# Opening of a fast-weight layer in another order on four engines, with the router's choice woven into its first steps

## The reference, cut to what matters

```python
xn = _layernorm(x)
xq, xk, xv = xn @ wq, xn @ wk, xn @ wv            # 16 heads of 64, chunks of 64 tokens
# for each chunk, state W and bias bb carried along:
lr = sigmoid(xk_c @ theta + tb);  eta = token_eta * lr / HD
Z1 = xk_c @ W + bb;  x_hat = (Z1 - mu) / std
grad_output = g * x_hat + be - (xv_c - xk_c)
Wn, bn = W - dW, bb - db                          # from eta and the gradient through the norm
out = xq_c + g * norm(xq_c @ Wn + bn) + be
# experts: softmax over tokens, the 32 strongest tokens of each expert
logits = einsum('bsd,de->bse', xn, Wg) + bg;  vals, idx = top_k(softmax(logits, -2).T, 32)
```

## Time and profile before

| what | value |
|---|---|
| median of 3 runs | 970.23 us (970.03 to 971.91) |
| the profiled execution's own time | 971.49 us |
| its span, first to last instruction | 969.3 us |
| busy: PE, DVE, ACT, POOL | 894.1, 781.8, 555.2, 629.6 us |
| mean granted TensorE clock | 0.979 |

### The profile page before, as it was taken

One profiled execution on the slowest core, in us unless ns is written; L12 is line 12 of the kernel. 1 busy time (PEld: TensorE's weight loads), 2 busy tenths in 40 slices (PEclk: granted clock), 3 DMA queues, 4 the chain that ended last, 5 costly groups with the idle time before them and its releaser, 6 DMA issues.

```text
span 969.3 us, 19700 instructions
## 1 busy us (share of the span) xinstructions
PE 894.1 (92%) x7768; PEld 617.4 (64%) x7768; DVE 781.8 (81%) x1182; ACT 555.2 (57%) x828; POOL 629.6 (65%) x571
## 2 busy tenths in 40 slices
PE   1687999999998897799999999999999999999997
PEld 1555778777786677556556656656656656666664
DVE  7768988998897635787887897888798788888876
ACT  3453666666664361456657656666655765756663
POOL 3357887888885002777668669568767866955872
PEclk9998999999999899799999999999999999999999
DMA  8100000000000301211011102101211111220110
GB/s 224 29 2 1 2 2 3 2 3 2 3 3 1 88 2 62 58 44 64 21 45 64 65 19 69 64 4 61 66 31 55 64 36 32 74 75 20 45 50 23
DMA packets 24962, 38.25 MB, mean 39 GB/s; under 512 B 9316, under 2 KB 15480, under 8 KB 22824
## 3 DMA queue, kind: packets, MB, share of 16 engines
q1 hardware_dynamic: 23240, 34.74, 11.7%
q10 hardware_dynamic: 1632, 2.27, 0.8%
HBM read 28.29 MB, written 1.43 MB: 31 GB/s over the span
## 4 chain that ended last, share of the span: by engine, by line
PE 60%; DVE 18%; issue 11%; POOL 6%; ACT 3%; DMA 1%; SPq 0%; POOLq 0%; DVEq 0%
PE bank L1142 12%; PE bank L1144 10%; PE bank L1143 10%; DVE hdh L958 5%; PE bank L1406 3%; PE bank L1298 3%; PE quad L1437 3%; PE quad L1194 3%; DVE add L967 2%; DVE mx L951 2%; PE quad L1185 2%; POOL arena L1068 2%; PE quad L1342 2%; PE bank L1257 2%; POOL arena L1062 2%
## 5 line engine op out<-in xcount | busy, mean ns | idle before, releaser
L951 DVE TENSOR_REDUCE mx<-quad 128x4 f32<-128x2048 f32 x64 | 146.4, 2288 | 41.4 <-PE quad L1437 41.3
L1113 POOL CAST hdh<-xn 128x512 fp32r<-128x512 f32 x96 | 65.7, 685 | 138.3 <-ACT xn L620 138.3
L635 ACT ACTIVATE ex<-quad 128x2048 f32<-128x2048 f32 x64 | 120.6, 1885 | 58.7 <-PE quad L1447 58.7
L1115 POOL TENSOR_TENSOR hdl<-hd,hdh 128x512 fp32r<-128x512 f32 x96 | 129.9, 1353 | 7.7
L1115 POOL TENSOR_TENSOR hdl<-xn,hdh 128x512 fp32r<-128x512 f32 x96 | 128.6, 1339 | 7.7
L1142 PE MATMUL bank<-hdh,W2h 128*128 128x512 f32 x256 | 113.1, 442 | 6.3 <-DVE hdl L961 4.1
L620 ACT ACTIVATE xn<-bank,b1c 128x512 f32<-128x512 f32 x128 | 88.0, 687 | 35.2 <-POOL hdl L1115 18.7
L620 ACT ACTIVATE hd<-bank,b1c 128x512 f32<-128x512 f32 x112 | 77.0, 688 | 45.1 <-PE bank L1144 26.8
L1144 PE MATMUL bank<-hdl,W2h 128*128 128x512 f32 x256 | 100.7, 393 | 0.0
L1143 PE MATMUL bank<-hdh,W2l 128*128 128x512 f32 x256 | 100.5, 393 | 0.0
L1142 PE MATMUL bank<-cH,W1h 128*128 128x512 f32 x192 | 81.0, 422 | 0.7 <-DVE cL L978 0.7
(11 more groups left out here) (304 smaller groups left out, 2205.5 us busy)
## 6 DMA issues: line engine op xcount, KB each, us to landing
cwB<-gate_rows SPq DMA_DIRECT2D x16, 1024.0 KB, 4.7
kx<-kqh SPq DMA_DIRECT2D x32, 64.0 KB, 2.1
qx<-kqh SPq DMA_DIRECT2D x32, 64.0 KB, 2.1
ex<-in_L_ffn_W SPq DMA_DIRECT2D x1, 1024.0 KB, 5.7
kx<-kql SPq DMA_DIRECT2D x16, 64.0 KB, 2.1
qx<-kql SPq DMA_DIRECT2D x16, 64.0 KB, 2.1
rec<-rec_rows SPq DMA_DIRECT2D x32, 32.0 KB, 2.1
out<-fin SPq DMA_DIRECT2D x4, 256.0 KB, 2.3
```

The source lines that it names most:

```text
L635: act.activation(ex[:, t % 2, :, :], quad[:, :, :], ACT.Exp, scale=float(AD) ** -0.5).then_inc(ROUND["exps_ready"], 1)
L951: dve.tensor_reduce(mx[:, t, :, 0], quad[:, :, :], AX_X, ALU.max, negate=True).then_inc(ROUND["score_max"], 1)
L1113: pool.tensor_copy(hdh[:, m % RING, :], tile(n)).then_inc(ROUND["pool_split"], 1)
L1115: pool.tensor_tensor(hdl[:, m % RING, :], tile(n), hdh[:, m % RING, :], ALU.subtract).then_inc(ROUND["pool_split"], 1)
```

## The change

It touches nothing behind the fast-weight loop. In words:

- GpSimd: clears `wgP` at the start (VectorE did); multiplies `theta` first, as soon as theta and `wk` are loaded; subtracts `wkl` only once the layer norm is done; no longer writes half of `Wst`; multiplies `wu` by gamma only once VectorE has written all of `Wst`; copies the router's weights into `wgP` ahead of `wql`.
- VectorE: casts `pair` and `ones` ahead of the norm; theta's sum and the bias come before `Wst`, of which it writes all four batches; scaling of the rates (`rates_scaled`) moves behind xhat of step 0; the pieces of the choice move from the end of steps 0 to 3 to two places within steps 1 to 4, one behind `xhat` and one ahead of L795.
- ScalarE: two of the four key blocks move into steps 0 and 1; the square root's table is loaded right behind the sigmoid and right behind the exponential, each by a one-element activation; the exponential moves from step 1 to step 2.
- TensorE: the same two key blocks move into steps 0 and 1; the router's logits go to `bank[0]` and wait for `wgP` alone; the turning of `wq` moves from step 0 to step 1 and waits for `choice(0)`; the turning of the ranks moves from step 4 to step 5; the first state products wait for `Wst` by halves.

The core of the diff:

```diff
             act.wait_ge(gamma_loaded, 16)
             act.activation(gg[:, :], gamB[:, :], ACT.Square, scale=HD ** -0.5).then_inc(wu_high, 1)
-            act.wait_ge(wu_ready, 2)
-            act.activation(wuh[:, :], wu[:, :], ACT.Copy, scale=1.0 / HD).then_inc(wu_high, 1)
...
-            for m in range(4):
-                keys(m, m + 1, second_bank if m % 2 else first_bank)
+            keys(0, 1, first_bank)
             act.wait_ge(bias_placed, 1)
             act.activation(Bhl[:, :], db_[:, :], ACT.Copy).then_inc(bias_first_high, 1)
+            keys(1, 2, second_bank)
+            act.wait_ge(wu_ready, 2)
+            act.activation(wuh[:, :], wu[:, :], ACT.Copy, scale=1.0 / HD).then_inc(wu_high, 1)
...
             act.activation(eta[:, :, :, :], eta[:, :, :, :], ACT.Sigmoid).then_inc(rates_sigmoid, 1)
-            act.wait_ge(target_ready, 1)
+            act.activation(warm[:, :], C("ln_eps"), ACT.Sqrt)
...
+                if s == 2:
                     act.wait_ge(choice_step, 2)
                     act.activation(rkp[:, 1, :], lgt[:, :], ACT.Exp, bias=es[:, 0:1], accum_out=es[:, 1:2]).then_inc(choice_exp, 1)
-                if s == 2:
+                    act.activation(warm[:, :], C("ln_eps"), ACT.Sqrt)
...
             for s in range(4 * NC + 6):
-                centre(s - 1), sum_squares(s), sum_squares_q(s), rdev(s), xhat(s), rdev_q(s)
+                centre(s - 1), sum_squares(s), sum_squares_q(s), rdev(s), xhat(s)
+                if s == 0:
+                    rates_scaled()
+                elif s <= 4:
+                    choice(2 * s - 2)
+                rdev_q(s)
                 if s % 2:
                     bias_low((s - 3) // 2)
-                normed(s), rate_of(s - 1), gradient(s), update(s - 2), sum_gx(s), sum_gx_xhat(s)
-                if s == 0:
-                    choice(0), choice(1)
-                elif s == 1:
-                    choice(2), choice(3)
-                elif s == 2:
-                    choice(4), choice(5)
-                elif s == 3:
-                    choice(6)
+                normed(s), rate_of(s - 1), gradient(s), update(s - 2), sum_gx(s)
+                if 1 <= s <= 4:
+                    choice(2 * s - 1)
+                sum_gx_xhat(s)
...
                 if s == 0:
-                    pe.wait_ge(wg_ready, 1)
-                    pe.wait_ge(rates_biased, 1)
+                    pe.wait_ge(CHUNK["u_taken"], 1)
+                    features(first_bank, 2, 0, wkh, wkl).then_inc(CHUNK["keys_ready"], 1)
+                    pe.wait_ge(wg_ready, 2)
                     for b in range(B):
-                        last = pe.matmul(misc[0:BE, :], wgP[:, b, :], xnT[:, b * S:(b + 1) * S], start=(b == 0), stop=(b == B - 1))
+                        last = pe.matmul(bank[0][0:BE, :], wgP[:, b, :], xnT[:, b * S:(b + 1) * S], start=(b == 0), stop=(b == B - 1))
                     last.then_inc(choice_logits, 1)
+                if s == 1:
+                    pe.wait_ge(CHUNK["xk_taken"], 2)
+                    features(second_bank, 3, 0, wkh, wkl).then_inc(CHUNK["keys_ready"], 1)
+                    pe.wait_ge(choice_step, 1)
```

More of the change, by code:

```diff
@@ L537, in _ @@
                 if s == 0:
+                    keys(2, 3, first_bank)
+                if s == 1:
+                    keys(3, 4, second_bank)
                     act.wait_ge(wq_turned, 1)
@@ L655, in _ @@
             half_ = lambda t: t.unsqueeze(2).broadcast_to([P, 8, P])
+            dve.wait_ge(consts_loaded, 16)
+            dve.tensor_copy(pair[:, :], C("pair"))
+            dve.tensor_scalar(ones[:, :], ident, 0.0, 1.0, ALU.mult, ALU.add)
             for k in range(2):
@@ L677, in _ @@
                 dve.tensor_tensor(by_chunk(xtl, b), bank[b][:, :].rearrange("p (i c) -> p i c", c=K), by_chunk(xth, b), ALU.subtract).then_inc(CHUNK["tokens_low"], 1)
[L679 to L682, removed]
+            dve.wait_ge(theta_scaled, 1)
+            dve.tensor_reduce(Th[:, :], th[:, :].rearrange("p (h c) -> p h c", h=H), AX_X, ALU.add).then_inc(theta_ready, 1)
             dve.wait_ge(rows_loaded, 16 * 8)
@@ L687, in _ @@
             dve.tensor_tensor(b8, b8, mb[:, 1, :].unsqueeze(2).broadcast_to([P, 8, HD]), ALU.subtract).then_inc(bias_ready, 1)
-            dve.wait_ge(consts_loaded, 16)
-            dve.tensor_copy(pair[:, :], C("pair"))
-            dve.tensor_scalar(ones[:, :], ident, 0.0, 1.0, ALU.mult, ALU.add)
+            dve.wait_ge(w_mean_ready, 1)
+            for b in range(B):
+                dve.tensor_tensor(Wst[:, b, :, :], W1s[:, :, :], m0[:, 1, 0:NP].unsqueeze(2).broadcast_to([P, NP, HD]),
+                                  ALU.subtract).then_inc(weights_centred, 1)
+            dve.wait_ge(bias_first_high, 1)
+            dve.scalar_tensor_tensor(out=Bhl[:, :], in0=Bhl[:, :], scalar=C("low_minus"), in1=db_[:, :], op0=ALU.mult, op1=ALU.add).then_inc(bias_ready, 1)
             link(dve.scalar_tensor_tensor(out=gb2[:, 0, :], in0=gb2[:, 0, :], scalar=1.0 / HD, in1=gb2[:, 1, :], op0=ALU.mult, op1=ALU.mult))
@@ L693, in _ @@
             dve.tensor_tensor(gbr[32:33, :], gb2[32:33, 0, :], gbr[32:33, :], ALU.subtract).then_inc(target_ready, 1)
-            dve.wait_ge(bias_first_high, 1)
-            dve.scalar_tensor_tensor(out=Bhl[:, :], in0=Bhl[:, :], scalar=C("low_minus"), in1=db_[:, :], op0=ALU.mult, op1=ALU.add).then_inc(bias_ready, 1)
+            dve.wait_ge(small_loaded, 16 * 4)
+            link(dve.tensor_scalar(rate[:, :], alpha[:, :], C("token_rate"), 0.0, ALU.add, ALU.max))
+            dve.tensor_scalar(rate[:, :], rate[:, :], 1.0 / HD, None, ALU.mult)
             dve.wait_ge(wu_high, 2)
             dve.scalar_tensor_tensor(out=wul[:, :], in0=wu[:, :], scalar=1.0 / HD, in1=wuh[:, :], op0=ALU.mult, op1=ALU.subtract).then_inc(wu_low, 1)
[L698 to L703, removed]
-                last = dve.tensor_copy(wgP[:, b, b * E0:(b + 1) * E0], wg0[:, :])
-            last.then_inc(wg_ready, 1)
-            for j in range(4):
-                r = slice(32 * j, 32 * j + 32)
-                dve.tensor_copy(b3s[r, :], eb[r, 2, :].rearrange("p (g j) -> p j g", j=4)[:, j, :])
-            dve.wait_ge(small_loaded, 16 * 4)
-            link(dve.tensor_scalar(rate[:, :], alpha[:, :], C("token_rate"), 0.0, ALU.add, ALU.max))
-            link(dve.tensor_scalar(rate[:, :], rate[:, :], 1.0 / HD, None, ALU.mult))
             dve.wait_ge(rates_raw, 1)
@@ L1050, in _ @@
             pool.wait_ge(gamma_loaded, 16)
+            pool.wait_ge(weights_centred, B)
             pool.tensor_tensor(wu[:, :], wu[:, :], gamB[:, :], ALU.mult).then_inc(wu_ready, 1)
+            pool.wait_ge(moe_loaded, 16 * N_M)
+            pool.wait_ge(wg_ready, 1)
+            for b in range(B):
+                last = pool.tensor_copy(wgP[:, b, b * E0:(b + 1) * E0], wg0[:, :])
+            last.then_inc(wg_ready, 1)
             pool.wait_ge(wq_high, 1)
```

63 lines of the change are left out of this document (34 added, 29 removed).

## The result

The changed kernel takes 961.15 us (median of 4 runs, 955.78 to 961.82), the kernel before 970.61 in the same rounds; the ratio of the means is 0.9889 with a 95% interval of 0.9852 to 0.9926 (that of the medians is 0.990; the one run at 955.78 makes the difference). The profiled execution took 961.21 us, its span is 959.2 us. The prediction was 960.0, with 956.0 to 963.5 as its range.

A forecast was written before the change was run, and what follows sets the result against it. No engine was full; a chain of hand-overs bound it, with GpSimd products blocking VectorE. Norm -4.1, theta +2.1, rest of opening -7.2, then +1.7, -4.4 and +1.7 gave -10.2: 970.2 to 960.0 us, range 956.0 to 963.5.

The forecast's parts named there:

- Theta (+2.1): Opening: GpSimd's theta product starts first and blocks VectorE's second subtraction, a loss of 2.1 us.
- rival A: Opening: VectorE starts first at theta, so the 2.1 us loss is absent; 957.9 us (956 to 959), chance 0.30.
- The norm (-4.1): End of the layer norm: with `wkl` waiting, VectorE's last products take 1.29 instead of 5.43 us, a gain of 4.1.
- The rest of the opening (-7.2): Opening apart from theta and norm: a gain of 7.2 us, with xhat of step 0 at 41.5 instead of 50.7.
- the two further blocks foreseen: Opening: VectorE held by GpSimd's gamma product for 1.4 us, and `wul` by `wql` for 2.2 us.
- GpSimd's four copies: Opening: copies into `wgP` between 30.1 and 32.2 us, free up to 2.1 us; if longer, `wul` precedes `wql`.
- a free GpSimd product: Opening: a GpSimd product over 1024 columns by itself, taken as 2.2 us.
- The table load: Opening, ScalarE: 1.3 us without the page's drain; by the page xhat of step 0 would come 1.4 us later.
- Step 0 to 1 (+1.7): Keys and logits wait for ScalarE's target copy; 1.7 us lost, the gain falling from 9.2 to 7.5.
- Rival B: Steps 0 and 1: TensorE stays at 1.2 GHz, xhat of step 1 at 55.5 not 52.2; 963.3 us, chance 0.17.
- Steps 1 to 5 (-4.4, +1.7): From xhat of step 1: moving the choice gains 4.4 us; step 4 to 5, with scan and passes new, loses 1.7.

The follow-up runs named there:

- wkl_early: The changed kernel with GpSimd's `wkl` no longer waiting for the norm: 962.6 us, 0.9921 of the kernel before.
- wql_late: The changed kernel with GpSimd's `wql` waiting until VectorE's `wul` is made: 957.0 us, 0.9852 of the kernel before.
- wst_gpsimd: The changed kernel with half of `Wst` (last two batches) back on GpSimd, TensorE's first state products waiting for all of it: 959.8 us, 0.9896 of the kernel before.
- logits_twice: The changed kernel with the router's logits computed twice in a row: 962.0 us, 0.9917 of the kernel before.
- choice_old: The changed kernel with VectorE's pieces of the choice back at the end of steps 0 to 3: 961.4 us, 0.9918 of the kernel before.
- mean_first: The changed kernel with GpSimd's `wkl` waiting for L680 (the mean of W1) instead of the norm: 958.0 us, 0.9864 of the kernel before.
- before_wait: The kernel before with only GpSimd's `wkl` made to wait for the norm: 971.5 us, 1.0006 of the kernel before.
- theta_late: The changed kernel with GpSimd's theta product also waiting for VectorE's second subtraction: 959.2 us, 0.9883 of the kernel before.
- before_choice5: The kernel before with choice and exponential placed as in the change, TensorE's turning of the ranks and ScalarE's copy in step 5: 964.4 us, 0.994.
- all_three: The changed kernel with theta behind VectorE's second subtraction, `wkl` behind L680, `wql` behind `wul`: 953.5 us, 0.9831 of the kernel before.

## Why the prediction was right

**Theta (+2.1).** Right in place and size (3.28 less 1.22 is 2.1). That it fell as forecast was luck: with the same code up to this point, GpSimd was first in five profiles (changed, wkl_early, wql_late, wst_gpsimd, logits_twice) by 0.01 to 0.14 us, and VectorE in two (choice_old by 0.10 us; mean_first, where theta landed 1.2 us behind VectorE's start). So rival A's mechanism exists; whether the changed kernel's one run of 955.8 us is such a case, its time alone doesn't tell.

**The norm (-4.1).** Right to the tenth, and wkl_early undid it. But before_wait shows that it is worth nothing alone. That it pays here because the other products were moved and thinned out as well fits the rows of before_wait, but no run divides the two.

**The rest of the opening (-7.2).** It was -6.3: xhat of step 0 came at 42.4 and not 41.5. The mis-sized step is "`wkl` then runs to 21.6 beside VectorE's `xtl`, which reads PSUM": ahead of `xtl` stands L680 with an SBUF input, which waited 1.7 us, so `xtl` ended at 23.8 and not 22.5. mean_first shows it. The Trainium skill, "SBUF — State Buffer", section "Who interferes with whom", counts `tensor_scalar` and `cast` among the VectorE instructions that can, under conditions on their operands, take the ports shared with GpSimd, and this trace agrees (1.90 us for L680). I had asked only for two inputs in SBUF. Of the two further blocks foreseen, 1.4 and 2.2, the profile has 1.4 and 1.7 (2.57 and 2.93 us less a free 1.2). GpSimd's four copies took 2.07 us and `wql` still began ahead of `wul`, as assumed. The 2.2 us that I took for a free GpSimd product was a little short: it measured 2.34 to 2.37, and the earlier trace rows already had 2.35.

The table load again took 1.28 us and the next activation started 1.30 us after it (38.59, 39.89), so the figure of the trace held. The 2.66 us that the Trainium skill, "ScalarE: Activation LUTs", section "What ACT_TABLE_LOAD costs", gives for a load with its drain were not seen here either.

**Step 0 to 1 (+1.7).** It gave back 1.6: 10.63 us, from 9.04. The logits ran mostly at the lower level (5.75 us; the forecast had 4.9, and 0.8 for just that). With the same code they took 4.6 to 6.0 us in the other profiles (4.59 in choice_old, 5.99 in theta_late), so the close fit owes something to chance. logits_twice confirms the chain. Rival B's price did not come, but its place did.

**Steps 1 to 5 (-4.4, +1.7).** Forecast 7.7, 8.1, 9.6 and 10.0, measured 7.4, 8.8, 8.8 and 9.7: 34.8 us against 35.4. Two misses cancel in it. Step 2 to 3 took 0.7 us more: VectorE stood 1.10 us for ScalarE's root, with TensorE's output-weight products (3.7 us, 60.56 to 64.29) ahead of step 3's operands, for which the forecast had 0.4. Step 3 to 4 took 0.8 less: GpSimd's `wog` did hold `scaled` back, to 2.1 us behind xhat (71.43), but VectorE's own passes covered that, and it was not idle ahead of the gradient. The sum of the gains at step 5 is 10.0 against 10.2.

**Which part pays.** The parts don't add. The placement of the choice alone gives 5.6 us (before_choice5), the rest alone 0.8% (choice_old, 961.4), both 1.1%. The last two intervals overlap, so that the placement adds anything in the new opening is not shown by the times; by the marks of one profile each it takes 1.8 us off steps 0 to 5 (47.2 against 45.4 us). The traces fit this: in the old opening, step 0 to 1 falls from 9.04 to 7.09 us when the choice leaves it; in the new one it takes 9.94 us with the choice in it and 10.63 without (9.68 in all_three, whose logits took 4.78 us), since TensorE's keys and logits bound it and the choice was hidden there. How much of the 1 to 2 us between single medians is theta's toss, and how much where the lower clock falls, stays open: the changed kernel's own runs spread from 955.8 to 961.8, and a single profile per kernel doesn't divide them. So I compare the parts by xhat and not by medians.

## What to carry to other kernels

Where GpSimd and VectorE both read SBUF, lay their rows side by side and ask for each GpSimd product which VectorE instruction starts just behind it; moving it only helps if it lands beside PSUM reads or idle time, and small instructions count too. A part of a change may be worthless or harmful alone and still be needed by the rest: follow each moved producer to its consumer on an in-order engine. Once the long stalls are gone, three one-line waits found by such a reading took another 6.3 us off the start of step 8's `xhat` (109.7 to 103.4), and the median came down from 961.2 to 953.5 in other rounds. Since the tail behind step 8 takes 847.7 to 851.4 us in these fourteen profiles with the same work in it, gains of 1 or 2 us in an opening are better read from a mark just behind it than from the total.
